# Four scan operations per chunk instead of six, joint roots, a new order of steps and output products by quarters in the second part of a four-layer kernel

## What is computed

```python
# third layer: q, k, v have 16 heads of 8 channels, beta is one number a head
def step(Sm, inp):                       # Sm: 8 x 8 for each of 8 x 16 heads
    qi, ki, vi, bi = inp
    Sk = einsum('bhkv,bhk->bhv', Sm, ki)
    Sm = Sm + bi * ki[..., :, None] * (vi - Sk)[..., None, :]
    return Sm, einsum('bhkv,bhk->bhv', Sm, qi)
h = x + scan(step).out @ Wo              # 512 steps one after another
y = rmsnorm(h, ln2)
x = norm(x + h + silu(y @ Wg) * (y @ Wu) @ Wd)          # "x3"
# fourth layer
g = silu(x @ w1) * (x @ w2)
g = gelu(gelu(g @ h1) @ h2)
out = norm(x + g @ w3)                                  # "x4"
```

## Time and profile before

| | |
|---|---|
| median of 3 runs | 1373.09 us (1367.09 to 1374.86) |
| the profiled execution | 1367.92 us, of which 1366.2 us is the span of its instructions |
| busy over the whole span | PE 86%, DVE 68%, ACT 46%, POOL 33% |
| part two | from 845 us to the end |
| one step in the middle of part two | 53.6 us |
| mean clock granted to PE | 0.944 of full |

### The profile page before, as it was taken

One profiled execution on the slowest core, in us unless ns is written; L12 is line 12 of the kernel. 1 busy time (PEld: TensorE's weight loads), 2 busy tenths in 40 slices (PEclk: granted clock), 3 DMA queues, 4 the chain that ended last, 5 costly groups with the idle time before them and its releaser, 6 DMA issues.

```text
span 1366.2 us, 19874 instructions
## 1 busy us (share of the span) xinstructions
PE 1170.0 (86%) x6173; PEld 616.5 (45%) x6173; DVE 926.2 (68%) x2401; ACT 623.3 (46%) x1194; POOL 453.3 (33%) x466
## 2 busy tenths in 40 slices
PE   5989889999899998989896751178999999999997
PEld 2434355453554544635444430134555545455453
DVE  3536536657587677776775577988988988898321
ACT  2071743736737447375373410213464454545642
POOL 3031311212333143232333233236446445544510
PEclk8999999999999999999999885579999999999999
DMA  3212030130321414114213168121020220200000
GB/s 99 82 47 71 1 109 9 48 94 33 109 65 42 131 32 134 47 29 138 55 35 67 25 149 200 48 49 44 14 65 19 47 65 8 57 24 8 24 8 8
DMA packets 85756, 79.91 MB, mean 58 GB/s; under 512 B 42800, under 2 KB 63408, under 8 KB 83632
## 3 DMA queue, kind: packets, MB, share of 16 engines
q1 hardware_dynamic: 85680, 79.01, 21.6%
HBM read 43.17 MB, written 35.00 MB: 57 GB/s over the span
## 4 chain that ended last, share of the span: by engine, by line
PE 50%; DVE 25%; ACT 10%; issue 9%; POOL 4%; DMA 1%; SPq 0%; ACTq 0%; DVEq 0%; POOLq 0%
PE ps L1305 10%; PE ps L954 5%; PE ps L1288 5%; DVE arena L1808 4%; ACT arena L1442 4%; PE ps L991 4%; PE ps L923 4%; ACT arena L1404 3%; PE ps L957 3%; PE ps L964 3%; PE ps L980 2%; DVE arena L2075 2%; PE ps L1058 2%; DVE ps L2070 2%; DVE arena L2073 2%
## 5 line engine op out<-in xcount | busy, mean ns | idle before, releaser
L1808 DVE TENSOR_REDUCE arena<-ps 128x4 f32<-128x512 f32 (+2 forms) x192 | 197.8, 1044 | 89.4 <-PE ps L957 86.3
L1305 PE MATMUL ps<-arena,late 128*128 128x512 f32 x512 | 224.5, 592 | 0.0
L1404 ACT ACTIVATE arena<-ps 128x512 f32<-128x512 f32 (+2 forms) x200 | 109.7, 567 | 232.6 <-PE ps L923 105.4
L1442 ACT ACTIVATE arena<-ps 128x1024 f32<-128x1024 f32 (+3 forms) x256 | 169.9, 711 | 30.6 <-PE ps L980 29.5
L753 POOL TENSOR_SCALAR_AFFINE_SELECT arena<-arena 128x512 f32<-128x512 f32 x128 | 82.9, 650 | 291.9 <-ACT arena L1442 290.4
L964 PE MATMUL ps<-mask_qk,ident_b 128*128 128x512 bf16 x505 | 137.6, 390 | 31.2 <-DVE arena L2087 31.1
L1305 PEld LDWEIGHTS ps<-arena,late 128*128 128x128 f32 x512 | 96.2, 190 | 115.8 <-issue 114.1
L1591 ACT ACTIVATE arena<-ps,f_s 128x512 f32<-128x512 f32 x128 | 85.2, 688 | 102.9 <-PE ps L1305 93.9
L1288 PE MATMUL ps<-arena,late 128*128 128x512 f32 x256 | 116.6, 609 | 7.8 <-ACT arena L1591 7.3
L848 POOL TENSOR_TENSOR arena<-arena 128x512 f32<-128x512 f32 x64 | 81.7, 1276 | 120.8 <-DVE slot_T L2104 76.5
L1404 ACT ACTIVATE arena<-ps,arena 128x128 f32<-128x128 f32 (+1 forms) x128 | 62.3, 528 | 124.5 <-DVE arena L1835 49.3
(11 more groups left out here) (186 smaller groups left out, 1960.7 us busy)
## 6 DMA issues: line engine op xcount, KB each, us to landing
qr<-q_rep SPq DMA_DIRECT2D x8, 1024.0 KB, 5.6
kr<-k_rep SPq DMA_DIRECT2D x8, 1024.0 KB, 7.9
scan_d<-late SPq DMA_DIRECT2D x56, 138.0 KB, 3.0
arena<-scan_d SPq DMA_DIRECT2D x12, 552.0 KB, 7.2
q_rep<-hilo SPq DMA_DIRECT2D x24, 256.0 KB, 3.3
k_rep<-hilo SPq DMA_DIRECT2D x24, 256.0 KB, 3.8
proj_d<-arena SPq DMA_DIRECT2D x8, 768.0 KB, 5.1
late<-proj_d SPq DMA_DIRECT2D x8, 768.0 KB, 4.5
```

The source lines that it names most:

```text
L1305: last = pe.matmul(ps[:, ring2.bank(f"{n}{c}"), :], w[:, k, c * P:(c + 1) * P], src[:, k, :], start=(k == 0), stop=(k == HC - 1))
L1404: return act.activation(dst, src(ps[:, bank, :]), func, **kw)
L1442: act.activation(prob[:, gg % 2, 2 * pr:2 * pr + 2, p_off[jt]:p_off[jt] + w], ps[:, bank:bank + 2, 0:w], ACT.Exp).then_inc(p_taken, 1)
L1808: v.tensor_reduce(heads[:, 2 * pr:2 * pr + 2, gs[0]:gs[-1] + 1], ps[:, at:at + 2, 0:len(gs) * w].rearrange("p q (n w) -> p q n w", w=w), X ...
```

## The change

Only part two changes. Five things:

1. **The scan has 4 operations a chunk.** `live` moves from PSUM into SBUF, as a fifth column of `k_u`, so that the sum over 4 and the addition of the state become one reduction over 5. The values, negated, stand as a ninth column in `w_s`, so that the sum over 8 and the subtraction become one reduction over 9 with `negate=True`. ACT writes the negated values, one small copy per quarter (`negate_v`, 32 in all), after `keep_history`; DVE waits for it once a quarter.
2. **Joint roots.** The roots of h and of x4 are taken together, 8 numbers wide instead of twice 4 (`roots`), so x4's root stands after the squares of h.
3. **New order on DVE**: the sums of the output products come first in a step, then x4's addition and moments, then `residual_h` after 28 scan operations of 64. In step 1 alone, `norm_x3` of tile 0 stands within the scan, after 56 operations, instead of after it.
4. **New order on PE**: `project_o` follows `layer_m` 0, `turn_h` follows `layer_m` 2 (in the first such step 2 and 3), and `turn_x3` stands in the middle of `last_out`. Idle matmuls are 32, 20 and 26 instead of 32, 28 and 56; the three before each `gates_ab` go.
5. **POOL makes the second half's products by quarters**: the third quarter's 8 products as soon as it is kept, the fourth's after `norm_x3`; before, the 8 products of the whole half came then.

The core of the diff:

```diff
-        live = [ps[:, 6 + k, 0:QUARTER * HD * HD]... for k in range(2)]
+        w_s = [c2.take(QUARTER * HD, CH, HD + 1) for _ in range(2)]
+        k_u = [c2.take(QUARTER * HD, HD, CH + 1) for _ in range(2)]
+        live = [tile[:, :, :, CH].rearrange("p (c v) d -> p c v d", v=HD) for tile in k_u]
+        v_neg = [tile[:, :, :, HD].rearrange("p (c v) j -> p c v j", v=HD) for tile in w_s]
...
-                    for half in range(2):
+                    for q, n in ((0, 2), (2, 1), (3, 1)):
                         for r in range(CH):
-                            out_products(scan, h, half, r)
+                            out_products(scan, h, q, n, r)
...
+                for k in range(HC):
+                    if last is not None:
+                        layer_m(last, turn, k)
+                    if mlp is not None and k == o_at:
+                        project_o(mlp, turn)
+                        if last is None:
+                            idle_matmuls(20, 5)
+                    if mlp is not None and k == h_at:
+                        turn_h(mlp, turn)
...
-                    yield o.mark(v.tensor_reduce(now_u[:, at, :, :], w_s, X, ALU.add))
-                    yield o.mark(v.tensor_tensor(now_u[:, at, :, :], wc[:, c, :, HD:2 * HD]..., now_u[:, at, :, :], ALU.subtract))
+                    yield o.mark(v.tensor_reduce(now_u, w_s[half][:, rows, :, :], X, ALU.add, negate=True))
...
-                    yield o.mark(v.tensor_reduce(ku_sum, k_u, X, ALU.add))
-                    yield o.mark(v.tensor_tensor(after[:, (c + 1) % QUARTER, :, :], now[:, at, :, :], ku_sum, ALU.add))
+                    yield o.mark(v.tensor_reduce(after[:, (c + 1) % QUARTER, :, :], k_u[half][:, rows, :, :], X, ALU.add))
...
+                if early_x3:
+                    upto(AT_X)
+                    norm_x3(mlp, 1 - h, Order(v, ln3_done, DVE_LN, mlp, CREDIT))
...
-AT_Y, AT_N, AT_H, AT_S = 4, 18, 34, 84
+AT_Y, AT_H, AT_X, AT_S = 4, 28, 56, 52
```

## The result

Interleaved with the kernel before on the same chip, the changed kernel took **1387.5 us** (median of 13 runs, 1378.9 to 1400.7) against 1372.1 us (13 runs, 1367.1 to 1390.5). The ratio is 1.012, 95% interval 1.010 to 1.014: **slower by 1.2%**. The forecast was 1361.5 us, range 1345 to 1373, with 0.08 for slower. It was wrong by 26 us and on the wrong side. The ratio leaves out executions in a slower state of the chip, of which the changed kernel's 1400.7 is one.

A forecast was written before the change was run, and what follows sets the result against it. PE and DVE were both taken as nearly the bound in the middle of part two, DVE alone at its start. Gains of 7.0 and 4.6 us, 11.6 of 1367.9, gave 1356.3 profiled and 1361.5 us as median, range 1345 to 1373.

The forecast's parts named there:

- The chunk: Scan on DVE: a chunk falls from 2.35 to 1.93 us, saving 6.7 us a tile, 54 us in eight.
- the middle: Six steps of part two, five with a scan: 321.1 us becomes 316.5, a gain of 4.6 us.
- costed at nothing: ACT's 32 negations, joint roots, POOL's 8 more instructions a tile, SP's transfers (5 us to spare) and the end: no cost.
- The wait for POOL: Scan's first multiplication, now with two SBUF inputs, waits for POOL's running instruction: about 0.15 to 0.4 us, bounds 0 and 1.1.
- The 0.065 us that fixed costs might have given: First multiplication of the scan, by the skill's fixed costs for SBUF and PSUM: about 1 us a tile, left unused.
- PE's floor: PE's middle step: turn_h saves 1.0 us and turn_x3 in last_out 1.1, so 53.6 becomes 51.5 us.
- Is DVE early enough: DVE's residual_h at F + 25.3 to 27.8, so PE waits 0 to 2.5 us at turn_h, 1.5 taken; step 53.0 us.
- F: The time at which mlp_out ends on PE, from which the prediction counts times within a step.
- Rival C: PE waits over 3 us at turn_h and its clock falls; a step lasts 57.2 us, total 1384 us; chance 0.08.
- s: PE's wait at turn_h in a middle step: between 0 and 2.5 us, taken as 1.5.
- The start: First steps of part two: gates_ab of tile 0 comes 11.4 us sooner, of tile 1 7.0 us sooner.
- rival D: The start gain melts (low clock after a longer wait ahead of turn_x3, POOL's quarter) and s = 2.5: 1370 us; chance 0.10.

The follow-up runs named there:

- kernel 7: The changed kernel with residual_h after 20 scan operations of 64 (5 chunks) instead of 28 (7 chunks): 1372.9 us, ratio 1.000 to the kernel before.
- kernel 1: The kernel before with live in SBUF, its 8 numbers side by side, and the sum over 4 in PSUM: 1395.8 us, ratio 1.019.
- kernel 8: The changed kernel with live back in PSUM, 5 operations a chunk, and residual_h after 25 scan operations of 80: 1355.4 us, ratio 0.987 to the kernel before.
- kernel 4: The changed kernel with live back in PSUM, 5 operations a chunk, residual_h still after 7 chunks: 1379.9 us, ratio 1.005 to the kernel before.
- kernel 2: The kernel before with live in SBUF as a column of rows of 5 (stride 5): 1426.1 us, ratio 1.040.
- kernel 3: The changed kernel with k_u turned, so live lies side by side and the sums read at a stride of 8: 1405.6 us, ratio 1.023 to the kernel before.
- kernel 5: The kernel before with the scan of 4 operations alone, old order and POOL by halves: 1384.6 us, ratio 1.010.
- kernel 12: The changed kernel with 10 idle matmuls ahead of turn_h in the five middle steps: 1382.2 us, ratio 1.006 to the kernel before.

## Why the prediction was wrong, point by point

**The chunk: the step that failed.** I left the first multiplication "at 0.42", since in size and kind it was the operation of before, and looked only at what contention would add. It reads a column of a tile, and that costs 0.20 us each, 3.2 us a tile. The chunk came to 2.14 us, not 1.93, so the saving was half of 6.7 us before the first wait. This is the term of the sum that was mis-sized. By itself it explains a part of the miss: from `norm_x3` to `residual_h` it is 1.4 us a step, and 3.4 us in scan 0. The rest of the way to 17.0 us in the middle is a late norm, the clock, and waits that I had costed at nothing, all of which follow below. The condition I gave for the first multiplication, "0.42 us with POOL idle", is the line that showed it.

**The wait for POOL: right in kind, and a little too high in size.** A mean of 0.10 us in the changed kernel (I had 0.15 to 0.4), the longest 0.85; small norm operations up to 1.27 us. In kernel 7 it is 0.16, and in the old order, where POOL works by halves, 0.2 to 0.27. The rule that I cited for it (the Trainium skill, SBUF — State Buffer, Who interferes with whom) holds here in its other half too, that a reduction never waits: L2093 stays within 0.442 and 0.464 us. The 0.065 us that fixed costs might have given, and that the sum left out, did not appear: the shortest first multiplication is 0.406 us with both inputs in SBUF (kernel 1) and 0.403 with one in PSUM (before).

**PE's floor: right.** 51.5 forecast; 50.86 measured in the last step of the changed kernel, and 50.86 to 51.13 in four of the six steps of kernel 8 (the other two, 52.0 and 52.95, have a wait of 0.62 and 1.31 us for the turned o ahead of `project_o`). PE's slot for `turn_h` came 31.1 us after the end of `mlp_out` (forecast 30.2), and from `residual_h` to `turn_h` it is 5.0 us (4.9).

**Is DVE early enough: the failed chunk at work.** In the step shown, F is 1215.01. `norm_x3` ended at F + 8.8 instead of 7.2, `residual_h` began at F + 29.4 instead of 25.3 to 27.8. Seven multiplications at 0.2 more are 1.4 us of that, 1.6 come in with the late norm. I took a wait of 1.5 us out of 0 to 2.5; the five were 1.67 to 3.34. DVE did wait for POOL ahead of `norm_x3`, as I had said (3.9 us, ending at 1208.68), but I had not seen that a late `turn_h` lengthens that wait: with `residual_h` two chunks earlier most of it is gone (kernel 7).

**What I never asked** is why `residual_h` had to stand there. My own terms put it at F + 25.3 to 27.8, and in the changed kernel it came at F + 29.4; `project_o` was through at F + 24.2, at 1239.2. Five chunks instead of seven take some 4.5 us from ahead of it, and kernels 7 and 8 have no wait at `turn_h` in the middle steps. I treated the order as given and priced only what happened in it.

**Rival C was the mechanism.** PE waits about 3 us at `turn_h`, and twice the clock falls (1.7 us each). That its 1384 us come near the 1387.5 is partly luck: it had 2.5 us for the clock in all five steps, so a middle 4 us too long, and 5 us kept at the start where nothing was kept. Its bound, "from s of about 3 on", was not sharp: the clock fell after a wait of 2.46 us at 1136.86, ahead of which PE had waited 1.31 and 1.19 us as well, and not after one of 3.10 at 1023.63; in kernel 1 it fell after 0.91 us and then 0.77. Its chance of 0.08 was too small because s was built from a chunk with no term for the unknown length of an operation that the trace of before does not contain, though its operands had changed.

**The start.** From the first multiplication to `gates_ab` of tile 0 it took 88.8 us instead of 95.7, 6.9 sooner, where I had 11.4. Of the missing 4.5, 3.6 were missing at `turn_h` of tile 0 already, which came 3.8 us sooner instead of 7.4; by its size that is the missing half of scan 0's saving, 3.4 us. Another 0.7 is `norm_x3` of tile 0 beside POOL, 8.7 us instead of 8. Of the 6.9 nothing was kept at tile 1, where I had 7.0. Here rival D's reason is at work: with 26 idle matmuls instead of 56 PE waits 4.96 us ahead of `turn_x3` of tile 0 (1.80 before), and `gates_ab` takes 9.56 us instead of 7.13.

```profile
940.09 1.11 PE L1275 MATMUL ps<-ident,arena 128*128 128x128 f32 x4 [4.96 <-ACT arena L1626]
941.89 9.56 PE L1292 MATMUL ps<-arena,late 128*128 128x512 f32 x16 [0.69 <-ACT arena L1593]
```

The granted clock from 941.89 to 951.50 is 0.74. `gates_gu` of tile 1 is slow too, 8.83 us, after a wait of 1.68 at `turn_h`.

**Costed at nothing.** ACT's copies of live take 0.666 instead of 0.383 us and the negations 0.437 where I had under 0.3; neither shows as a wait of its own (DVE waits 5.8 us for `keep_history` in the changed kernel and 5.3 us in kernel 4, whose copies are short). SP's transfers did not have 5 us to spare everywhere: PE waited 0.94 and 1.19 us for the turned o in two of the five middle steps.

## What to carry to other kernels

An operation whose count of elements stays the same is still a new operation when its operand becomes a column of a wider tile: price the access pattern, on both the reader and the writer, before taking an operation out to make room for it. When a kernel on several engines gets a new order, ask of every hand-over how long its input has been ready before it is taken; here 5 us lay idle between `project_o` and `residual_h`, and one number was worth 14.7 and 24.5 us, against 18.5 for all that kernel 8 gains over the kernel before. And a change that loses need not be all bad: the new scan alone lost 1.0%, the new order alone 2.4%, both together 1.2%, and the new order with a scan shortened without the stride and `residual_h` two chunks earlier gains 1.3%.

## What the runs showed of the hardware

- A DVE multiplication of 256 elements of 4 bytes takes 0.42 us with its input from SBUF side by side (kernel 1) and 0.62 with that input at a stride of 5 elements (kernel 2). Writing at a stride of 8 costs 0.18 us, and a reduction over 320 elements read at it takes 0.73 instead of 0.49 (kernel 3). ACT's copy of 256 goes from 0.415 to 0.667 us at the stride of 5.
- Two inputs in SBUF cost nothing by themselves (0.406 us), only beside a running POOL instruction, then up to 1.1 us. The mean wait is 0.20 to 0.27 us in the old order with products by halves (kernels 1, 2, 5) and 0.10 to 0.16 in the new order with the second half by quarters (changed, 3, 7, 12); whether the shorter instructions or the order do that is not shown.
- The clock of PE fell from the 2.4 GHz level after a wait of 3.34 us (changed kernel) and after two of 0.91 and 0.77 (kernel 1), and not after one of 3.10 (changed kernel). The length of one wait did not decide it here. Ten idle matmuls in the wait (kernel 12) kept it at 1.00.
